# Peeling the last pair of slot steps and extracting the top entries in one block, in a four-layer graph network on one core

## What is computed

```
L0: d = (sum|adj| + eps)^-0.5;  elu(adj @ ((h @ W) * d) * d + b)
L1: att = sigmoid(left_i + right_j) * adj
    out = expmap(h, sum_j att_ij * logmap(h_i, h_j))        # atanh and norms for each pair i,j
L2: msg_ij = gelu(layernorm(h_j @ W1a + h_i @ W1b + b1) * g1 + be1)
    agg_i  = sum_j adj_ij * msg_ij                          # the costly one: only where adj_ij != 0
    layernorm(concat(h, agg) @ W2 + b2)
L3: four layers tanh(concat(src_agg, self, dst_agg) @ wu + bu) on the l2-normalised adjacency
```

## Time and profile before

| what | value |
|---|---|
| median of 3 runs | 4009.07 us (4004.93 to 4012.15) |
| profiled execution | 4007.12 us, its span 4005.3 us |
| busy: DVE, PE, ACT, POOL | 3267.3, 3231.7, 2663.1, 1939.6 us |
| mean granted clock of PE | 0.913 of 2.4 GHz |
| chain that ended last, by engine | issue 27%, PE 20%, POOL 19%, DVE 19%, ACT 9%, DVEq 3% |
| slot steps | 310, in 16 groups (L581 x310) |

### The profile page before, as it was taken

One profiled execution on the slowest core, in us unless ns is written; L12 is line 12 of the kernel. 1 busy time (PEld: TensorE's weight loads), 2 busy tenths in 40 slices (PEclk: granted clock), 3 DMA queues, 4 the chain that ended last, 5 costly groups with the idle time before them and its releaser, 6 DMA issues.

```text
span 4005.3 us, 92223 instructions
## 1 busy us (share of the span) xinstructions
PE 3231.7 (81%) x24743; PEld 2745.1 (69%) x24840; DVE 3267.3 (82%) x11961; ACT 2663.1 (66%) x6659; POOL 1939.6 (48%) x1598
## 2 busy tenths in 40 slices
PE   3484688787888889788788888888897887888888
PEld 2273667677676777767677776767777676776777
DVE  4788888888888888888888888888888888887830
ACT  2484776848667585766848676685857668495753
POOL 1182753719355382744718273461827447182730
PEclk7596889999899999989999998999999899999999
DMA  2010102012020210202011020202102020110200
GB/s 82 29 53 29 50 9 75 24 36 73 5 79 16 67 37 30 72 3 80 24 51 48 30 68 2 83 22 62 37 30 72 4 80 24 41 46 9 61 8 21
DMA packets 147064, 167.74 MB, mean 42 GB/s; under 512 B 13232, under 2 KB 100912, under 8 KB 146736
## 3 DMA queue, kind: packets, MB, share of 16 engines
q1 hardware_dynamic: 146736, 163.96, 13.5%
HBM read 151.33 MB, written 12.58 MB: 41 GB/s over the span
## 4 chain that ended last, share of the span: by engine, by line
issue 27%; PE 20%; POOL 19%; DVE 19%; ACT 9%; DVEq 3%; POOLq 1%; ACTq 0%; DMA 0%; SPq 0%
POOL v_z L570 13%; PE n_bank_c L1604 4%; PE n_bank_d L1621 3%; PE n_bank_d L1622 3%; POOL v_prstd L581 2%; PE n_bank_d L1618 2%; DVE v_top_at L1077 2%; POOL v_pvar L578 2%; PE n_bank_b L1679 2%; ACT v_rows L813 1%; DVE v_top L1074 1%; DVE v_normed L1168 1%; ACT v_pair L878 1%; DVE v_adj_x L1082 1%; PE n_bank_b L1835 1%
## 5 line engine op out<-in xcount | busy, mean ns | idle before, releaser
L570 POOL TENSOR_TENSOR v_z<-v_z,all_bc_L_gnn_be 128x512 f32<-128x512 f32 x620 | 787.1, 1271 | 50.5 <-DVE v_z L1128 24.2
L781 ACT ACTIVATE v_diag<-all_ident,v_value 128x128 f32<-128x128 f32 x2480 | 754.0, 386 | 0.0
L1522 PE MATMUL n_bank_d<-v_diag,v_msg 128*128 128x128 f32 x4960 | 637.8, 283 | 31.0 <-ACT v_diag L781 29.9
L1522 PEld LDWEIGHTS n_bank_d<-v_diag,v_msg 128*128 128x128 f32 x4960 | 594.3, 196 | 36.7 <-ACT v_diag L781 32.9
L581 POOL TENSOR_TENSOR v_prstd<-v_pvar,all_neg_half 128x8 f32<-128x8 f32 x310 | 578.9, 1868 | 25.8
L1513 PE MATMUL n_bank_b<-v_parts,v_onehot 128*128 128x128 f16 x5472 | 379.9, 227 | 181.1 <-ACT n_bank_b L730 180.9
L1513 PEld LDWEIGHTS n_bank_b<-v_parts,v_onehot 128*128 128x128 f16 x5472 | 327.4, 101 | 236.1 <-ACT n_bank_b L730 231.2
L1604 PE MATMUL n_bank_c<-all_l_wsd,v_fT 128*128 128x256 f32 x1792 | 449.6, 393 | 29.3 <-ACT v_adjT L715 26.8
L1513 PE MATMUL n_bank_c<-v_parts,v_onehot 128*128 128x128 f16 x4960 | 339.2, 224 | 131.8 <-ACT n_bank_c L730 131.1
L725 ACT ACTIVATE v_fT<-n_bank_d,all_l_c 128x256 f32<-128x256 f32 x256 | 119.9, 474 | 462.3 <-PE n_bank_d L1622 462.1
L1128 DVE SCALAR_TENSOR_TENSOR v_z<-n_bank_c,v_prstd,all_bc_L_gnn_g 128x128 f32<-128x128 f32 x1240 | 345.3, 342 | 89.5 <-POOL v_prstd L581 89.4
(11 more groups left out here) (277 smaller groups left out, 6617.3 us busy)
## 6 DMA issues: line engine op xcount, KB each, us to landing
v_spread<-slot_rows SPq DMA_DIRECT2D x342, 256.0 KB, 3.2
v_adj_l<-in_adj SPq DMA_DIRECT2D x128, 256.0 KB, 4.0
v_adj_x<-in_adj SPq DMA_DIRECT2D x64, 256.0 KB, 3.7
v_ring<-in_x SPq DMA_DIRECT2D x16, 512.0 KB, 5.6
out_x<-v_xout SPq DMA_DIRECT2D x64, 128.0 KB, 1.9
slot_rows<-v_indexT SPq DMA_DIRECT2D x16, 256.0 KB, 2.0
w_wu<-in_L_gnn_wu SPq DMA_DIRECT2D x4, 192.0 KB, 2.5
all_W<-in_L_gnn_W SPq DMA_DIRECT2D x2, 128.0 KB, 4.0
```

The source lines that it names most:

```text
L570: nc.gpsimd.tensor_tensor(z[par][:, units], z[par][:, units], wide(bc["L2_gnn_be1"])[:, units], ALU.add).then_inc(sem["z_ready"], 1)
L781: ins = nc.scalar.activation(diag[par][:, u], ident[:], ACT.Copy, scale=value[:, u, bass.ds(slot, 1)])
L1522: ins = nc.tensor.matmul(ps_agg[:, u // NB, (u % NB) * P:(u % NB + 1) * P], msg[par][:, u], diag[par][:, u], start=False, stop=False, skip ...
```

## The change

Four things are done.

1. `keep_slots` stores the number of slots less two, so that a register `body` stands where `pairs` stood and the last pair of steps is written out behind the loop on SP, ACT, DVE and PE (POOL keeps its loop with `body + 1` pairs). In what is written out, work for slots past the last is left out: for each group two `pick`s (two instructions each) and their two spread DMAs, one gather with its two seeds, and DVE's wait for that gather. The number of slot steps of a group is as before.
2. ACT's last `diagonals` stands ahead of `gelu(1, after, 0)`.
3. The extraction is one block of 8 units with `ratios` behind its first round; `clip` comes behind all of it and behind `index_ready`.
4. The number of rounds is `(S + 7) // 8`, where S is the number of slot steps, and was `(S + 10) // 8`. For 18 and 20 steps both give 3, for 22 steps 3 in place of 4. Only group 3 has 22 steps; its extraction lies in mix 2.

```diff
@@ SP @@
-                n = sp.value_load(n_slots[0:1, bass.ds(a, 1)], min_val=7, max_val=N)
-                sp.reg_mov(n_pairs, (n + 1) // 2)
+                n = sp.value_load(n_slots[0:1, bass.ds(a, 1)], min_val=7, max_val=N - 2)
+                sp.reg_mov(n_body, (n + 1) // 2)
...
-                with sp.Fori(2, pairs + 1) as i:
+                with sp.Fori(2, body + 1) as i:
@@ POOL @@
-                pairs = pool.snap((n + 1) // 2)
+                pairs = pool.snap((n + 1) // 2 + 1)
@@ ACT @@
-                def act_step(par, step, slot, second=False):
-                    act.wait_ge(sem["z_made"], step * 2 + 1)
-                    seed(1 - par, 0)
+                def act_step(par, step, slot, second=False, last=False):
+                    if not last:
+                        act.wait_ge(sem["z_made"], step * 2 + 1)
+                        seed(1 - par, 0)
...
-                act.reg_add(count, count, pairs * 2)
+                act.reg_add(count, count, body * 2)
+                ending = act.snap(count)
+                for par in range(2):
+                    act_step(par, act.snap(ending + par), act.snap(body * 2 + par), last=par == 1)
+                act.reg_add(count, count, 2)
                 after = act.snap(count)
                 gelu(0, act.snap(after - 1), 1)
+                diagonals(1, after, act.snap(body * 2 + 1))
                 gelu(1, after, 0)
-                diagonals(1, after, act.snap(pairs * 2 - 1))
                 gelu(1, after, 1)
@@ DVE @@
-                v.tensor_scalar(n_slots[0:1, bass.ds(a, 1)], needed_g[:], 7.0, float(N), ALU.max, ALU.min)
+                v.tensor_scalar(needed_g[:], needed_g[:], float(N), -2.0, ALU.min, ALU.add)
+                dve.drain()
+                v.tensor_scalar(n_slots[0:1, bass.ds(a, 1)], needed_g[:], 7.0, None, ALU.max)
...
-                full = dve.snap(((n + 1) // 2 * 2 + 10) // 8 - 1)
+                full = dve.snap(((n + 1) // 2 * 2 + 9) // 8 - 1)
...
-                if between:
-                    between()
+                between()
...
-                    pick(dve.snap(step + g * 2 + 2), par)
+                    if not last:
+                        pick(dve.snap(step + 2), par)
...
-                dve.wait_ge(sem["gathered"], (after + g) * 2 + 2)
...
-                    take_slots(a, 0)
-                    ratios()
-                    take_slots(a, 1, between=clip)
+                    take_slots(a, between=ratios)
                     dve.drain().then_inc(sem["index_ready"], 1)
+                    clip()
@@ PE @@
-                def pe_step(par, step, slot, first=False, second=False):
-                    ahead = pe.snap(step + g * 2 + 2)
-                    pe.wait_ge(sem["onehot_ready"], ahead)
-                    gather(1 - par, pe.snap(step + g + 1), 0)
-                    gather(1 - par, pe.snap(step + g + 1), 1)
+                def pe_step(par, step, first=False, second=False, last=False):
+                    if not last:
+                        pe.wait_ge(sem["onehot_ready"], step + 2)
+                        gather(1 - par, pe.snap(step + 1), 0)
+                        gather(1 - par, pe.snap(step + 1), 1)
```

More of the change, by code:

```diff
@@ L454, in second_spreads @@
             def second_spreads(a):
-                before = sp.snap(sp.snap(count) + a * 2)
+                before = sp.snap(count)
                 for par in range(2):
@@ L461, in slots @@
             def slots(a):
[L462 to L464 removed]
+                body = sp.snap(n_body)
+                before = sp.snap(count)
+                with sp.Fori(2, body + 1) as i:
                     for par in range(2):
@@ L1059, in keep_slots, with take_slots @@
                 dve.drain()
-                v.tensor_scalar(n_slots[0:1, bass.ds(a, 1)], needed_g[:], 7.0, float(N), ALU.max, ALU.min)
+                v.tensor_scalar(needed_g[:], needed_g[:], float(N), -2.0, ALU.min, ALU.add)
+                dve.drain()
+                v.tensor_scalar(n_slots[0:1, bass.ds(a, 1)], needed_g[:], 7.0, None, ALU.max)
                 dve.drain().then_inc(sem["slots_ready"], 1)
[L1063 to L1066, removed]
+            def take_slots(a, between):
+                for b in range(GB):
@@ L1074, in eight @@
                         v.max(top[:, u], adj_x[:, u])
                     dve.drain()
-                    for u in units:
+                    for u in range(UNITS):
                         v.max_index(top_at[:, u], top[:, u], adj_x[:, u])
-                    v.tensor_copy(value[:, these, bass.ds(r * 8, 8)], top[:, these])
+                    v.tensor_copy(value[:, :, bass.ds(r * 8, 8)], top[:])
                     dve.drain()
                     if more:
-                        for u in units:
+                        for u in range(UNITS):
@@ L1130, in normalise, with dve_step @@
                     ins.then_inc(sem["z_made"], 1)
-                def dve_step(par, step, first=False):
+                def dve_step(par, step, first=False, last=False):
                     for half_ in range(2):
-                        dve.wait_ge(sem["gathered"], (step + g) * 2 + (half_ + 1))
+                        dve.wait_ge(sem["gathered"], step * 2 + (half_ + 1))
                         for two in range(half_ * (HALF // 2), (half_ + 1) * (HALF // 2)):
@@ L1539, in pe_step @@
                             aggregate(par, pe.snap(step - 1), half_)
-                pe_step(0, before, 0, first=True)
-                pe_step(1, pe.snap(before + 1), 1, second=True)
-                with pe.Fori(1, pairs) as i:
+                pe_step(0, before, first=True)
+                pe_step(1, pe.snap(before + 1), second=True)
+                with pe.Fori(1, body) as i:
                     for par in range(2):
-                        slot = pe.snap(i * 2 + par)
-                        pe_step(par, pe.snap(before + slot), slot)
-                pe.reg_add(count, count, pairs * 2)
+                        pe_step(par, pe.snap(before + (i * 2 + par)))
+                pe.reg_add(count, count, body * 2)
+                ending = pe.snap(count)
+                for par in range(2):
+                    pe_step(par, pe.snap(ending + par), last=par == 1)
+                pe.reg_add(count, count, 2)
                 after = pe.snap(count)
```

65 lines of the change are left out of this document (34 added, 31 removed).

## The result

| | before | with the change |
|---|---|---|
| median | 4010.61 us (4 runs, 4004.93 to 4014.43) | 3954.62 us (4 runs, 3952.95 to 3957.52) |
| profiled execution, span | 4007.12, 4005.3 | 3952.95, 3951.2 |
| 16 stretches of slots, sum | 1460.1 | 1428.9 |
| mixes 0 to 14, sum | 2152.2 | 2127.5 |
| up to the first slot step, behind the last | 214.2, 178.8 | 215.3, 179.4 |

A stretch of slots is counted from DVE's first scaling (L1128 before, L1133 after) to the end of the last; a mix is what lies between. Of the 54.1 us between the spans 31.2 came from the slots, where some 4 were forecast, and 24.7 from the mixes, where 8 were; the start and the end together lost 1.8.

A forecast was written before the change was run, and what follows sets the result against it. It took POOL to set the pace of the slots, and no engine to be always busy in a mix; terms -6.4, -3.9, +1.2, -1.3, -0.6, -1.3 and -2.7 sum to -15.0 from 4007.12: 3992 us, range 3968 to 3999.

The forecast's parts named there:

- the reading of the bound: In the slots, POOL's shifts follow its power with no idle time marked, so POOL sets the pace.
- the term for regular mixes: Extraction in one block, regular mixes: DVE's gain ends waiting for ACT's exponentials, so 0; bounds -0.7 and +0.7 each.
- rival B: At the nodes' transposes PE's clock stays up as DVE comes earlier: up to 15.6 won in 12 mixes, 3976; chance 0.12.
- What becomes of small gains: Mixes starting earlier lose much of it at PE's 1.2 GHz clock: of 8.3 us in 13 groups a third stays, -2.7.
- Rival A: Small gains add up: the clock's steps follow PE's work, all 8.3 us come through, 3986 or 3980; chance 0.22.
- rounds by need: Extraction in mix 2 drops its fourth round: -6.4 us, bounds -4.4 and -8.1.
- Powers: POOL's last two powers of each group lose the pick beside them: 0.22 shorter each, 0.44 a group, 7.0 in all.
- First mixes: Mixes -1 and 0 at the start gain from extraction in one block: -1.7 and -2.2, -3.9 together.
- Mix 14: In mix 14 clip comes later than ACT's logs began, so everything behind gets later: +1.2 us, bounds 0 and +2.
- Last group's sum: Diagonals ahead of the gelu end PE's last aggregate earlier: -1.3 us in the last group, -0.6 in mix 0.
- Rival D: Clip, behind 8 units' rounds, is late in every mix and delays ACT's logs: slower, 4018 us; chance 0.05.
- C: Rival: loop exits and written-out steps cost 0.5 us a group, first mixes gain nothing: 4004, no change; chance 0.08.

The follow-up runs named there:

- the drains: Kernel before with eight DVE drains put once between mix 0 and the loop over groups: 3993.1 us, ratio 0.9956.
- the swap: Kernel before with DVE's wait for the gelu's buffer written ahead of its wait for POOL's power in the slot step: 3969.8 us, ratio 0.9906.
- after_two_halves: Changed kernel with the old extraction put back (two halves, four rounds in mix 2, clip among the second half's rounds): 3981.3 us.

## Why the prediction was wrong

**The step that failed first** is the reading of the bound: "POOL's shifts at 752.36 begin as the power that began at 750.51 ends (752.39), with no idle time marked: POOL sets the pace of the slots." POOL had 0.09 us of idle time in each step, hidden in a row of several instructions, and waited in it for DVE, whose first scaling started 0.10 late for register arithmetic behind the wait. The change altered the form of a semaphore's value in each step, which the prediction did not cost. It measured -23.7 alone and +24.5 undone, and is the largest single part of the change. The sign stood in the rows before: DVE's scaling at 752.52 begins 0.13 behind the power's end.

**The second is the term for regular mixes**, "0; bounds -0.7 and +0.7 each". DVE's own gain was worked out well: from the first MAX8 to layer 0's part 37.4 us in mix 6 before and 36.65 after, 0.8 where 0.7 was forecast. But the forecast let it end at ACT's exponentials. DVE had not been held there before (no idle time ahead of L1033 in mix 6), so that B's counter-argument, "DVE is held at 1817.12 whatever comes before", was wrong; it gained about 0.2 and then waits 0.48. The pause at the transposes fell by 0.5, and the clock held in all regular mixes: rival B, given 0.12, with a price of 15.6 for 12 mixes. Measured are 1.7 us behind the transposes in each of the 12, 21, of which 19 are left over the whole mixes. But B came true in part by luck: some 0.3 of those 0.5 are a stall that went as code moved, which nobody forecast, and the drains show that this alone can hold the clock. Whether the extraction would have done it alone stays open; by the estimate above it would not. The term also stands twice: 0 here, and 0.2 for each mix (2.6) in the small gains.

**The third is "What becomes of small gains"**. The runs don't bear it out: the swap's slots gave 23.7, and its mixes, which all began earlier, gave none of it back: from the slots' end to the transposes mixes 1 to 13 took 128.9 on average, where they took 129.1 before and 129.5 with the drains, whose slots were the old ones. The 0.84 between mixes 6 and 9 shows that lengths of like mixes differ by about 1 us, not that they cancel a gain. Rival A had this right.

The other terms: **rounds by need** -6.4, measured -5.6 alone in the medians, and mix 2 of 144.2 where 144.5 was named. **Powers** 0.44 for each group: 1.65 instead of 1.88, right; 7.4 for 16 groups. **First mixes** -3.9 with mix 0's sum -0.6 besides: mix 0 gave 2.4, but the first slot step came 1.2 later; over all kernels it lies between 210.9 and 215.9, so mix -1's term can't be told. **Mix 14** +1.2: it measured +3.7, of which ACT's wait for clip is 2.0. **Last group's sum** -1.3: PE's sum came 0.8 earlier in mixes (DVE's wait in the last group 11.47, was 12.25), and putting the diagonals back changed nothing. That in the mixes the gain is lost at ACT's squares was right. **Rival D** did not happen but in mix 14, **C** nowhere.

## What to carry to other kernels

Where an engine seems to set the pace, add its instructions up one by one over a period (here 2 x 1.27 + 0.20 + 1.87 and the gaps) and compare with the period; a merged row, and an idle total larger than its named part, can hide a wait that runs through another engine. Between a wait on the critical path and the instruction behind it nothing should be left to compute: write the wait that ends last as the last one, with its value in a register. And ask of a pause of PE not only how long it is but what its clock does behind it: a few tenths of a us of another engine's work decided over 1.6 us, thirteen times. Before a gain of under 0.5% in a long program is given to an edit, add instructions that do nothing outside of the loop and see how much the time moves by that alone (here 16 us).

## What the runs showed of the hardware that I had not expected

Register arithmetic between a wait and DVE's next instruction delays that by 0.10 us (0.13 against 0.03 behind the power's end). Idle time put down to "issue" of 0.35 us and more at one instruction comes and goes with instructions added elsewhere, the same in each pass of the loop: 0.49 to 0.14 with eight drains outside of it. PE's clock at the transposes held in all mixes but one where the mean pause was 1.21 to 1.27 (the exception had 1.44), in 8 of 13 at 1.29, and in none or one of 13 from 1.44 on (the one is mix 2: 1.57 in the kernel before, 1.21 in after_two_halves).
